# Four mixed layers on one core: order at the seam of the channel heads and the third mixture, and the list of routed tiles made another way

## The reference

```python
x = x + tanh(g_xattn[i]) * attention_i(layernorm(x), ctx)
x = x + tanh(g_ffn[i]) * ffn_i(layernorm(x))
```

```python
masked = jnp.where(emask > 0, biased, -jnp.inf)   # 2 of 4 groups of experts allowed
_, sel = jax.lax.top_k(masked, TOP_K)
w = jnp.take_along_axis(scores, sel, axis=1)
w = w / (w.sum(-1, keepdims=True) + 1e-20)
...
y = silu(x @ g.T) * (x @ u.T) @ d.T               # per expert, weighted and summed
```

## Time and profile before

| | |
|---|---|
| median of 3 runs | 1431.4 us (1430.3 to 1447.9) |
| profiled execution, its own time | 1438.35 us |
| its span | 1436.6 us |
| TensorE busy | 1144.2 us (80%), mean granted clock 0.883 |
| VectorE, ScalarE, GpSimd busy | 781.3, 502.0, 565.3 us |

### The profile page before, as it was taken

How to read it: one execution, slowest core, us unless ns; L and a number is a source line. 1 busy time by engine, 2 the same in 40 slices (tenths; PEclk the granted TensorE clock), 3 DMA queues, 4 the chain that set the end, 5 groups by cost and what they waited for, 6 DMA issues and landing times. The chain is left out here.

```text
span 1436.6 us, 25477 instructions
## 1 busy us (share of the span) xinstructions
PE 1144.2 (80%) x7228; PEld 822.1 (57%) x7229; DVE 781.3 (54%) x2794; ACT 502.0 (35%) x1336; POOL 565.3 (39%) x854
## 2 busy tenths in 40 slices
PE   5377975499999993799986889967996786699970
PEld 4255764287777772466655766624554444577750
DVE  5857434222444444687845545576777634655547
ACT  0254210012333330466652134413674431144430
POOL 4651056500333333665562324412221556355550
PEclk9998887599999996899998899956999956899995
DMA  9599932201333337111010224344000112255547
GB/s 398 153 301 287 340 120 87 76 16 33 106 108 107 106 102 288 60 48 57 2 43 30 80 77 135 105 143 172 1 2 1 47 65 88 87 148 151 147 136 263
DMA packets 92378, 169.37 MB, mean 118 GB/s; under 512 B 11287, under 2 KB 70825, under 8 KB 91305
## 3 DMA queue, kind: packets, MB, share of 16 engines
q1 hardware_dynamic: 72585, 107.63, 24.4%
q0 software_dynamic: 17664, 48.91, 9.5%
q10 hardware_dynamic: 2043, 11.75, 2.0%
HBM read 82.64 MB, written 85.61 MB: 117 GB/s over the span
## 5 line engine op out<-in xcount | busy, mean ns | idle before, releaser
L2071 PE MATMUL bank<-weights,xT 128*128 x832 | 241.4, 413 | 1.9 <-ACT xT L2159 1.7
L1914 POOL DMA_INDIRECT slots_out<-weights,y_rows x128 | 122.7, 959 | 166.1 <-DVE y_rows L2313 105.7
L2071 PEld LDWEIGHTS bank<-weights,xT 128*128 128x128 f32 x832 | 142.4, 191 | 27.8 <-issue 4.0
L1908 POOL DMA_INDIRECT slots_in<-xn_wide,row_in x114 | 112.4, 986 | 113.7 <-DMA slots_in<-xs_wide 50.8
L1914 POOL DMA_INDIRECT slots_out<-pack,y_rows x80 | 76.5, 956 | 194.8 <-DVE y_rows L2313 186.2
L2159 ACT COPY xT<-bank 128x256 f32<-128x256 f32 x208 | 77.5, 373 | 120.8 <-PE bank L2063 100.6
L1403 PE MATMUL bank<-ctx,weights 32*128 32x256 f32 x512 | 78.4, 448 | 37.5 <-DVE weights L1511 22.3
L2013 PE MATMUL bank<-weights,rows 128*128 128x256 f32 x256 | 75.2, 413 | 34.9 <-DVE x L2263 18.5
L1457 ACT ACTIVATE weights<-bank 128x512 f32<-128x512 f32 x128 | 72.6, 597 | 71.3 <-PE bank L1411 66.1
L2255 DVE TENSOR_TENSOR rows<-rows,bank 128x256 f32<-128x256 f32 (+1 forms) x56 | 22.5, 401 | 137.5 <-ACT rows L2141 109.7
L2290 DVE TENSOR_TENSOR weights<-weights,bank 128x128 f32<-128x128 f32 x128 | 36.8, 287 | 109.8 <-ACT weights L2163 98.5
(11 more groups left out here) (418 smaller groups left out, 2543.5 us busy)
## 6 DMA issues: line engine op xcount, KB each, us to landing
slots_in<-xs_wide SPq DMA_DIRECT2D x16, 2112.0 KB, 19.0
weights<-slots_in SPq DMA_DIRECT2D x96, 132.0 KB
xs_wide<-slots_in SPq DMA_DIRECT2D x72, 132.0 KB
rows<-slots_out SPq DMA_DIRECT2D x16, 512.0 KB, 3.4
xn_wide<-slots_out SPq DMA_DIRECT2D x16, 512.0 KB, 4.8
weights<-in_l_gu SPq DMA_DIRECT2D x1, 7040.0 KB
pack<-slots_in SPq DMA_DIRECT2D x40, 132.0 KB
weights<-in_l_gu ACTq DMA_DIRECT2D x1, 4608.0 KB, 14.5
```

Of the source, the lines that this page charges most:

```text
L1908: pool.indirect_dma_start(out=slots_in, in_=xn_wide[:, t, :], in_offset=None, out_offset=bass.IndirectOffsetOnAxis(ap=row_in[:, t, i:i + 1 ...
L1914: pool.indirect_dma_start(out=slots_out, in_=y[:, n % U, :], in_offset=None, out_offset=bass.IndirectOffsetOnAxis(ap=y_rows[:, n % U:n % U ...
L2071: last = nc.tensor.matmul(out, xT[:, n.c % 2, c, :], flat(gu_w[:, ds(e, 1), c, :]), start=(c == 0), stop=(c == C - 1 and layer != 2))
```

## The change

At the seam, group 1's count moves from step 15 to step 16, VectorE takes one routing step a slot in place of two, and the scatters inside the heads go from 6, 6, 6, 6, 4, 4 in steps 13 to 18 to 6, 6, 14, 6, 4 in steps 13 to 17, so that 12 in place of 16 stay for the mixture. In the third mixture all of choosing stands before the first chunk, and the count in chunk 1; in the second the count moves to chunk 3 and the pace from 5 to 3.

The list: rank_experts brings each expert's running sum and unused blocks onto that expert's own partition (16 partitions), makes two rows of comparisons there, and signals ranked. In chunk 40, 11 or 6 TensorE multiplies them by ones, which sums over the experts and spreads the sums to 128 partitions in a bank. list_tiles finishes from there. In mixtures 2 and 3 weigh_rows comes after the shared part, behind tiles_listed.

```diff
--- before.py
+++ after.py
@@ channel_heads
-            count_in = (11, 15)
-            scatter_in = {13: 6, 14: 6, 15: 6, 16: 6, 17: 4, 18: 4}
+            count_in = (11, 16)
+            scatter_in = {13: 6, 14: 6, 15: 14, 16: 6, 17: 4}
...
-                        for _ in range(g + 1):
-                            next(routing[g], None)
+                        next(routing[g], None)
@@ list_tiles, now rank_experts, ranks_of and list_tiles
-    def list_tiles(layer, dve, step, rt):
+    def rank_experts(layer, dve, step, rt):
...
-        big = rt["scores"][:, 0:8 * routed].rearrange("p (e n) -> p e n", e=8)
...
-        step(nc.vector.tensor_copy(mine, numbers[:, 0:routed]))
-        step(nc.vector.memset(owner, 0.0))
         yield
-        for h in range(2):
-            e = slice(8 * h, 8 * h + 8)
-            part = rt["part"][:, 0:routed]
-            step(nc.vector.tensor_tensor(big, numbers[:, 0:routed].unsqueeze(1).broadcast_to([P, 8, routed]),
-                                         cum[:, e].unsqueeze(2).broadcast_to([P, 8, routed]), ALU.is_ge))
-            yield
-            step(nc.vector.tensor_reduce(part, big.rearrange("p e n -> p n e"), AX.X, ALU.add))
-            step(nc.vector.tensor_tensor(owner, owner, part, ALU.add))
-            yield
-            step(nc.vector.tensor_tensor(big, big, spare[:, e].unsqueeze(2).broadcast_to([P, 8, routed]), ALU.mult))
-            yield
-            step(nc.vector.tensor_reduce(part, big.rearrange("p e n -> p n e"), AX.X, ALU.add))
-            step(nc.vector.tensor_tensor(mine, mine, part, ALU.add))
-            yield
-        step(nc.vector.tensor_scalar(owner, owner, NE - 1.0, None, ALU.min))
+        own_column, column, past = ranks_of(rt)
+        step(nc.vector.tensor_tensor(own_column, rt["tiles"][0:NE, 1:3, :],
+                                     ident[0:NE, 0:NE].unsqueeze(1).broadcast_to([NE, 2, NE]), ALU.mult))
+        step(nc.vector.tensor_reduce(column, own_column, AX.X, ALU.add))
+        step(nc.vector.tensor_scalar(past[:, 0, 0:routed], numbers[0:NE, 0:routed], column[:, 0:1], None, ALU.is_ge))
+        step(nc.vector.tensor_scalar(past[:, 1, 0:routed], numbers[0:NE, 0:routed], column[:, 0:1], column[:, 1:2],
+                                     ALU.is_ge, ALU.mult))
+
+    def list_tiles(layer, dve, step, rt, LIST):
...
+        step(nc.vector.tensor_scalar(owner[0:1], LIST[0:1, 0, 0:routed], NE - 1.0, None, ALU.min))
+        step(nc.vector.tensor_tensor(mine, numbers[:, 0:routed], LIST[:, 1, 0:routed], ALU.add))
         step(nc.vector.tensor_scalar(mine, mine, NE * NB - 1.0, None, ALU.min))
+        yield
@@ mixture
+            list_at = {1: 40, 2: 11, 3: 6}[layer]
+            LIST = bank[6][:, 0:2 * ROUTED].rearrange("p (i n) -> p i n", i=2)
...
-                                              2: (((t0, NB),), (0,), (2,), 5), 3: (((t0, NB),), (0,), (2,), 4)}[layer]
+                                              2: (((t0, NB),), (0,), (3,), 3), 3: (((t0, NB),), (0,), (1,), 4)}[layer]
...
+                    if n == list_at:
+                        pe.wait_ge(ranked, 1)
+                        nc.tensor.matmul(LIST, ones[0:NE, :], ranks_of(rt)[2], start=True, stop=True).then_inc(listed, 1)
...
-                        yield from list_tiles(layer, dve, step, rt)
+                        yield from rank_experts(layer, dve, step, rt)
+                        dve.sem_inc(ranked, 1)
+
+                def listing():
+                    dve.wait_ge(listed, 1)
+                    yield from list_tiles(layer, dve, step, rt, LIST)
+                    if layer == 1:
                         yield from weigh_rows(layer, dve, step, rt)
-                        dve.sem_inc(tiles_listed, 1)
-
+                    dve.sem_inc(tiles_listed, 1)
...
+                if layer == 3:
+                    for _ in choice[0]:
+                        pass
...
-                for _ in placement[-1]:
+                    if n >= list_at:
+                        for _ in range(pace):
+                            next(lists, None)
+                    if n + 1 == list_at:
+                        for _ in placement[-1]:
+                            pass
+                for _ in lists:
+                    pass
+                for _ in weigh_rows(layer, dve, step, rt) if layer > 1 else ():
                     pass
@@ third_mixture
-            mixture(3, rt, carve, LAST, scattered, 16)
+            mixture(3, rt, carve, LAST, scattered, 12)
```

10 lines of the change are left out of this document (9 added, 1 removed).

## The result

| | before | after |
|---|---|---|
| median of the runs, us | 1431.9 (1430.3 to 1447.9, 4 runs) | 1455.0 (1450.8 to 1459.0, 4 runs) |
| ratio | | 1.0127, 95% interval 1.0082 to 1.0172 |
| profiled execution: span, us | 1436.6 | 1455.9 |

The account below looks back on a forecast made before the run. The start times of the three routed loops bound the kernel, limited by late instructions, VectorE's list, and late expert choice. First mixture -1, second -7, third -7 with the seam's delay: -15 from 1431.4, so 1416.4 us; range 1402 to 1434.

Parts of the forecast that it names:

- Starvation stays where it is, as nothing ahead of it moves: First mixture: late instructions during GpSimd's scatters cost the same after the change as before.
- so they are hidden: Heads, step 15: fourteen scatters in a row fit in GpSimd's 10.68 us of idle time and cost nothing.
- Nothing is waited for there; instructions come late: First mixture: TensorE's "issue" gaps, 16.3 us in one group, are late instructions, setting in 15.5 us into the scatters.
- in the second mixture's burst nothing starved: Second mixture, kernel before: TensorE did not starve in the burst of scatters, having run little of its code.
- First mixture, forecast -1: First mixture: a 1.3 us wait for x goes, 0.4 us for the list matmul comes: -1 us.
- starvation: Engines standing in long bursts of GpSimd's indirect DMAs, taken to be because instructions come late.
- Second mixture, forecast -7 (-13 without starvation): Second mixture: waits for x and low clock go, less a later first scatter, -13; 6 us of late instructions leave -7.
- Seam, forecast +7.8: Channel heads: late placement and scatters queued on GpSimd delay the last root; the stage ends 7.8 us later.
- Third mixture, forecast -14.8 from its own start: Third mixture: choosing first starts the loop sooner, halfway between no engine stands and TensorE starving in 28 scatters; -14.8 us.
- The third loop, forecast 0: Third mixture's loop over routed tiles keeps TensorE full and is left alone by the change: 0 us.
- Slower: GpSimd's queue at the seam decides: Rival, heads: four scatters waiting for placement delay roots, and the third loop starts late; +7, 1438.5 us, chance 0.14.
- No starvation: Rival, all mixtures: no engine lacks instructions in bursts; -1 - 13 - 13.4 = -27.4, 1404 us, chance 0.17.

Follow-up runs that it names:

- the quiet chip: Kernel before and whole change on a fifth chip, where engines hardly stand in GpSimd's bursts: 1348.2 and 1333.8 us, ratio 0.9913.
- list alone: Kernel before with only the new list of tiles from ranks, on the second chip: 1448.8 us, 0.9940 of before.
- pauses: Changed kernel with four small GpSimd copies after the fourth, ninth and last of step 15's fourteen scatters: 1455.0 us, 0.9999 of before.
- no queue: Changed kernel with two scatters in step 16, none in step 17, and 20 tokens' scatters left to the third mixture: 1468.8 us, 1.0070 of before.
- old seam: Changed kernel with the heads' count, scatters and routing steps as before: 1444.3 us, 0.9914 on the second chip; 1332.1 us, 0.9907 on the fifth.
- the last pair: Changed kernel, scatters spread in all mixtures, heads' seam as before or as changed, sixth chip: 1333.7 or 1339.6 us, 0.9889 or 0.9928.
- the kernel made for it: The new list with nine memsets on VectorE, on the fourth chip: 1335.6 us in its one execution.

## Why the prediction was wrong, by its steps

**The step that failed.** The forecast priced the stands in GpSimd's bursts too low: nothing in the first mixture ("Starvation stays where it is, as nothing ahead of it moves"), 6 us in the second, nothing in the heads ("so they are hidden"), and half of the gain in the third. By stages the result missed the forecast by 4.7, 11.4, 9.3 and 15.7 us, and the rest came out 6.7 us better: 34.4 in all. On the quiet chip the whole sum came out. There the kernel before takes 90 us less (1346.4 for 1436.6), 57 of them in the first mixture, and the changed kernel 125 less. So the change saves 15.2 us where engines hardly stand, and the stands give it 34.5 us more: together the +19.3.

**What bounds the kernel.** The stands were found in the right places, and bursts of scatters do bring them on: held back, they gave 52 us. But "Nothing is waited for there; instructions come late" was argued, and the traces speak against it: the instructions had been fetched, and ScalarE stood for signals that were recorded 10 us late and more. The prediction also has that in the second mixture's burst nothing starved; the kernel before takes 5.9 us more in that stage than on the quiet chip.

**First mixture, forecast -1.** Without starvation -1.3: right. With it +3.7. Its code ahead of that point is the same in the changed kernel and in four variants of it, and the six gave 350.6 (list alone), 352.1 (pauses), 355.2 (no queue), 356.2 (old seam), 355.4 and 356.1 (the changed kernel twice): a band of 5.6 us that nothing in the mixture's own code explains. The changed kernel gave 355.4 and 356.1 on two chips and the kernel before 351.7 and 352.4, so a kernel seems to keep its place in the band. What decides it wasn't found.

**Second mixture, forecast -7 (-13 without starvation).** Without starvation -9.0: the sum of what goes was too large by 4, as 4.6 us of the wait for x and the 1.6 before the loop remained, which I had both gone. With starvation +4.4, not -7. The forecast's 6 us for it were mis-sized. TensorE's stand came about when the prediction had it, 16.6 us into the burst (15.5), after ScalarE's first at 10.5 us. But it lasted 9.9 us, not 8, and the low clock came after it, 1.8 us for the eight matmuls shown. Between the chips the stage of the changed kernel differs by 19.4 us, that of the kernel before by 5.9. That TensorE gave the gain back because it now ran into the burst at full speed fits this, but isn't shown.

**Seam, forecast +7.8.** Without starvation +4.4 against before, and +8.6 against the kernel with the old seam (342.0 for 333.4), +9.6 in the last pair: the mechanism, late placement and GpSimd's queue, is right and about its size. With starvation +17.1 and +19.4. I had let the burst of sixteen cost nothing, "fourteen in a row in the 10.68 us in which it stood idle ..., so they are hidden"; hidden for GpSimd, not for the others. Undoing the seam took 18 us off this stage, three pauses 5. The same text put 3 us on it in the rival that came true in kind.

**Third mixture, forecast -14.8 from its own start.** Choosing first was right within 1.1 us: the placement came 12.1 us after the block's start on the quiet chip (1123.9 less 1111.8), for 13.2 foreseen, and the last scatter 34.5 us after it, for 35.4. The loop then starts when the loads land, 39.8 us after the block's start (41.4 foreseen), for 49.5 before: -9.7. The forecast had the start of before at 62.6, with ScalarE's 12.75 us stand in it as if it were the order's. On the quiet chip that stand isn't there. On the first chip the new order gave nothing (+0.9), and this is the largest miss of all: the forecast took the middle between no stand and one of 18 to 20 us, and TensorE stood 16.5 and 5.7 us.

**The third loop, forecast 0** ("which the change leaves alone"): -7.5 us on the first chip. Taken from one result scatter to the eighth after it, the second to fourth turn took 15.8 to 16.3, 14.2 to 14.9 and 14.5 to 14.8 us in the three traces of kernels with the old list on chips that starve, and 13.0 or 13.1 in the seven with the new. A slow stretch of before and one of after, 15 us each:

```profile
1303.00:1318.00 15.00, 13.94 (x74) 10.98 (x73) 7.81 (x40) 6.26 (x24) 7.69 (x8) 1.00 0.47 142
```

```profile
1302.00:1317.00 15.00, 15.00 (x85) 12.70 (x84) 8.54 (x45) 7.46 (x29) 8.63 (x9) 1.00 0.61 161
```

The first is of the unchanged kernel on the third chip. Quiet chips have 127.7 us for the loop in all kernels. So this too belongs to what the chips differ in; why the kernels with the new list have it better stays open, as the kernel made for it met a quiet chip.

**The rivals.** "Slower: GpSimd's queue at the seam decides", at 0.14 and 1438.5 us, had the place and the sign, with the burst starving TensorE as a part of it; its price was 17 us short. Its sum can't be redone either: +9 for the loop with -1 and -4 is +4, not +7. "No starvation", 1404 us, is the kernel on a quiet chip, but there the kernel before hardly starves either, so its -27.4 is -15.2. That the total on the quiet chips, -14 us, is so near to my -15 is chance: the second mixture and the seam came out 2.0 and 3.4 us below their terms, and the third mixture 4.6 us above.

## What to carry to other kernels

A row with "issue" or "remote" gaps on several engines at once, beside a burst of GpSimd's indirect DMAs, is a cost that a change can move, lengthen and also remove: let GpSimd wait on the progress of the engine that stands, one tile's scatters at a time. Before giving the cause a name, compare the recorded increment of the semaphore with the instruction that gives it, and the times of the instruction packets with the stands. Price each change with and without such stands, since what the order gains in a clean trace it can lose there. And measure before and after on the same chip and, where a trace shows such stands, on more than one: this change is 1.3 per cent slower in one measurement, no different on a second chip and 0.9 per cent faster on a third.

## What the runs showed of the hardware

The largest number of this study isn't of the change. The same kernel takes 1432, 1456 and 1460 us on three chips and 1349, 1348 and 1350 on three others. The traces differ in whether engines stand while GpSimd scatters, and in how many semaphore records they hold. From 200 to 220 us GpSimd issues 17 scatters on the quiet chip and 18 on the first, and DMA moves 102 to 104 and 104 to 108 GB/s; TensorE is busy 19.1 of the 20 us on the one and 7.8 on the other. The instruction queue q8 has the same 46 packets and 0.75 MB in both. Each of the five chips of the experiments served one group only, the two slow ones ahead of the three quiet ones, so the runs can't tell a difference of chips from one of time. What makes an execution one or the other, they don't show.

The Trainium skill, "Runtime: NRT & Kernel Launch", section "Instruction fetch mechanics", has the cost of crossing into the next block mostly hidden. The traces agree on both kinds of chip: on the first, packets of 16 KB at 302.7 and 325.7 us took 1.3 and 0.9 us while TensorE was busy without a gap (3.00 of 3 us around each), and the stands of the first mixture hold none from 200.1 to 257.4. The prediction read them as a contradiction, and they are none.

Pauses work even when very short: on the second chip gaps of 0.4 to 2.3 us between groups of four scatters were enough for TensorE to run without a stand from 253 to 283 us. On the same chip it still stood elsewhere: from 210 to 220 us it was busy 5.59 of 10.
